# A graph layer on one core: projections as three passes over 12-bit parts, inputs laid out transposed, the self projection kept in DRAM

## The reference

```python
Wi, Wj = W[:, :512], W[:, 512:]                 # W is 512 x 1024
mi = einsum('bkd,od->bko', x, Wi)               # x is 8 x 2048 x 512, float32
mj = einsum('bkd,od->bko', x, Wj)
a = adj.astype(float32)                         # adj is 2048 x 2048 int32, zeros and ones
deg = a.sum(axis=1)
out = deg[None, :, None] * (mi + b) + einsum('ij,bjo->bio', a, mj)
y = x + out
return (y - mean(y)) / sqrt(var(y) + 1e-5)      # over the last axis
```

## Time and profile before

| | |
|---|---|
| time, median of 3 runs (range) | 1845.88 us (1845.76 to 1846.46) |
| profiled execution, span from first to last instruction | 1843.9 us |
| what lies around the span (median less span) | 2.0 us |
| PE busy / DVE busy / ACT busy / POOL busy | 1826.7 / 1182.1 / 418.1 / 1.1 us |
| moved by DMA | 86.41 MB, 47 GB/s over the span |

### The profile page before, as it was taken

One profiled execution on the slowest core, in us unless ns is written; L12 is line 12 of the kernel. 1 busy time (PEld: TensorE's weight loads), 2 busy tenths in 40 slices (PEclk: granted clock), 3 DMA queues, 4 the chain that ended last, 5 costly groups with the idle time before them and its releaser, 6 DMA issues.

```text
span 1843.9 us, 20125 instructions
## 1 busy us (share of the span) xinstructions
PE 1826.7 (99%) x6352; PEld 1171.2 (64%) x6352; DVE 1182.1 (64%) x2704; ACT 418.1 (23%) x455; POOL 1.1 (0%) x8
## 2 busy tenths in 40 slices
PE   9999999999999999999999999999999999999998
PEld 5458854588545885458844688446884468844687
DVE  7755487645885558855588545875558844688454
ACT  4454410123001320022201222011220112211131
POOL 0000000000000000000000000000000000000000
PEclk9999999999999999999999999999999999999999
DMA  6530001100111001010101100010001100010001
GB/s 234 180 117 34 34 34 45 34 34 34 42 38 34 34 34 45 34 34 38 42 34 34 42 37 34 34 45 34 34 34 35 44 34 34 34 45 34 12 34 46
DMA packets 22765, 86.41 MB, mean 47 GB/s; under 512 B 2400, under 2 KB 3424, under 8 KB 20704
## 3 DMA queue, kind: packets, MB, share of 16 engines
q1 hardware_dynamic: 22752, 86.25, 12.9%
HBM read 52.69 MB, written 33.55 MB: 47 GB/s over the span
## 4 chain that ended last, share of the span: by engine, by line
PE 88%; DVE 9%; issue 2%; ACT 0%; DVEq 0%; DMA 0%; POOL 0%; POOLq 0%; SPq 0%
PE agg_ps L261 45%; PE mj_ps L243 21%; PE mi_ps L243 21%; DVE xT L402 5%; DVE stats L421 1%; DVE r L419 1%; DVE r L415 1%; PE aux_ps L234 0%; DVE r L410 0%; DVE newton L430 0%; PE mi_ps L304 0%; ACT std L340 0%; DVE mean_var L423 0%; DVE mj_top L388 0%; ACT WT L312 0%
## 5 line engine op out<-in xcount | busy, mean ns | idle before, releaser
L261 PE MATMUL agg_ps<-mj_hi,adjT 128*128 128x512 f32 x2048 | 799.7, 390 | 0.0
L261 PE MATMUL agg_ps<-mj_lo,adjT 128*128 128x512 f32 x2048 | 796.8, 389 | 0.0
L243 PE MATMUL mj_ps<-WT,xT 128*128 128x512 f32 x1024 | 461.9, 594 | 8.2 <-DVE xT L402 7.4
L243 PE MATMUL mi_ps<-WT,xT 128*128 128x512 f32 x1024 | 460.4, 592 | 0.8 <-ACT WT L312 0.8
L402 DVE STREAM_TRANSPOSE xT<-x_in 32x256 f32<-32x256 f32 x1008 | 439.2, 436 | 20.2 <-DMA x_in<-in_x 5.4
L261 PEld LDWEIGHTS agg_ps<-mj_hi,adjT 128*128 128x128 f32 x2048 | 384.4, 188 | 81.3 <-issue 1.7
L261 PEld LDWEIGHTS agg_ps<-mj_lo,adjT 128*128 128x128 f32 x2048 | 384.4, 188 | 81.3 <-issue 1.7
L334 ACT ACTIVATE adjT<-adjT 128x2048 fp32r (+1 forms) x128 | 244.4, 1915 | 548.1 <-PE agg_ps L261 548.0
L243 PEld LDWEIGHTS mi_ps<-WT,xT 128*128 128x128 f32 x1024 | 194.5, 190 | 245.5 <-issue 238.9
L243 PEld LDWEIGHTS mj_ps<-WT,xT 128*128 128x128 f32 x1024 | 192.1, 190 | 246.5 <-issue 245.3
L419 DVE TENSOR_TENSOR r<-agg_ps,r 128x512 f32 (+1 forms) x128 | 88.5, 691 | 345.9 <-PE agg_ps L261 345.4
(11 more groups left out here) (28 smaller groups left out, 172.6 us busy)
## 6 DMA issues: line engine op xcount, KB each, us to landing
x_in<-in_x SPq DMA_DIRECT2D x63, 512.0 KB, 3.3
out<-r SPq DMA_DIRECT2D x63, 512.0 KB, 2.6
stage<-in_adj SPq DMA_DIRECT2D x16, 1024.0 KB, 5.1
stage<-in_L_gnn_W SPq DMA_DIRECT2D x2, 512.0 KB, 5.2
stage<-in_L_gnn_W SPq DMA_DIRECT2D x1, 1024.0 KB, 9.4
x_in<-in_x SPq DMA_DIRECT2D x2, 256.0 KB, 4.6
out<-r SPq DMA_DIRECT2D x2, 256.0 KB, 2.0
bias<-in_L_gnn_b SPq DMA_DIRECT2D x1, 256.0 KB, 9.5
```

The source lines that it names most:

```text
L243: last = nc.tensor.matmul(dst[u % 2][:, :], xT[u // 2][:, u % 2, k, :], WT[:, half * DK + k, :], start=(k == 0), stop=(k == DK - 1))
L261: last = nc.tensor.matmul(agg_ps[s][:, :], adjT[s][:, j, :], part[:, j, :], start=(j == 0 and part is mj_hi), stop=(j == NT - 1 and part i ...
```

## The change

**Projection.** `x`, W and their parts are handled in 12-bit pieces. For a tile, `x_top` is the upper bits of x, `x_hi` the same as fp32r, `x_lo` is 4096 times the rest, and `x_df = x_top - x_lo`; for W the parts are `W_hi`, `W_lo` and `W_df`. A product is then `main * (1 + 1/4096) - cross`, where `main` sums `x_hi * W_hi` and `x_lo * W_lo` (8 matmuls) and `cross` sums `x_df * W_df` (4 matmuls). All operands are fp32r, so `mj` and `mi` of a tile take 24 matmul instructions. DVE makes the top and the rest (`split_x`) and combines (`combine_mj`, `combine_mi`); ACT makes `x_hi` and `x_lo` (`parts`), copies `cross` out of PSUM (`take_cross`) and makes `mj_hi`; POOL makes `x_df` (`difference`) and `mj_lo` (`rest_of_mj`). `x_top`, `mj` and `mi` have one buffer each.

**Layout.** The host hands over `x` once as it is and once transposed by tile (`xt`), `adj` transposed in blocks of 128 x 512 (`adjt`, 64 chunks) and W transposed (`wt`, 8 chunks). No engine transposes any more. Of the chunks of `adj`, 32 are handled in the projection stage of batch 0, two a tile, and 32 in its aggregation stage: 3 in each of tiles 1 to 4, 2 in tiles 5 and 6, 4 in tiles 7 to 10. DVE counts the degrees of each chunk and ACT casts it.

**Self projection.** `mi` is stored to `mi_dram` a tile at a time and read back in the aggregation stage, where POOL adds the bias (`add_bias`) and DVE forms `r = mi * deg + x` (`residual`). `r` now has four single-tile buffers, and `x` is read a second time into them. All transfers are of 256 KB and all are issued by SP.

In the cut below the new parts come in the order SP, POOL, PE, ACT, DVE, host.

```diff
-            def project(n, u, dst, half, free, ready, wait_free):
...
-                    last = nc.tensor.matmul(dst[u % 2][:, :], xT[u // 2][:, u % 2, k, :], WT[:, half * DK + k, :],
-                                            start=(k == 0), stop=(k == DK - 1))
-                last.then_inc(ready, 1)
...
-            def transpose_pair(q, slot, quadrants, slot_value):
...
-                for a in quadrants:
-                    blocks = x_in[slot][a * B:(a + 1) * B, :, :].rearrange("p s (k g c) -> p s k g c", g=Q, c=B)
-                    for g in range(Q):
-                        last = nc.vector.transpose(xT[slot][g * B:(g + 1) * B, :, :, a * B:(a + 1) * B],
-                                                   blocks[:, :, :, g, :])
...
-            def residual(n, t, u):
-                dve.wait_ge(mi_ready, n + 1)
-                nc.vector.scalar_tensor_tensor(slot(r, t), mi_ps[u % 2][:, :], deg[:, bass.ds(t, 1)],
-                                               x_in[u // 2][:, u % 2, :], ALU.mult, ALU.add).then_inc(r_ready, 1)
...
-                nc.vector.scalar_tensor_tensor(slot(r, i), bias[:, :], deg[:, bass.ds(i, 1)], slot(r, i),
-                                               ALU.mult, ALU.add).then_inc(degb_ready, 1)
...
+            def load_chunk(c):
+                s = c % 2
+                if c >= 2:
+                    sp.wait_ge(adj_cast, c - 1)
+                    sp.wait_ge(deg_part_ready, c - 1)
+                sp.dma_start(adj_in[s][:, :], adjt[c // NT, c % NT]).then_inc(adj_loaded[s], 16)
+            sp.dma_start(x_raw[0][:, :], xt[0]).then_inc(x_loaded[0], 16)
+            for c in range(DK, 2 * DK):
+                sp.dma_start(w_stage[c][:, :], wt[c]).then_inc(w_loaded[c], 16)
+            sp.dma_start(x_raw[1][:, :], xt[1]).then_inc(x_loaded[1], 16)
+            for c in range(DK):
+                sp.dma_start(w_stage[c][:, :], wt[c]).then_inc(w_loaded[c], 16)
...
+            def load_mi(m, u):
+                sp.dma_start(mi_in[u % 2][:, :], mi_dram[m]).then_inc(mi_loaded[u % 2], 16)
+            def load_r(m, u, turn):
+                if turn is not None:
+                    sp.wait_ge(out_stored[u], turn)
+                sp.dma_start(r[u][:, :], x_tiles[m]).then_inc(r_loaded[u], 16)
...
+                def proj(g):
+                    for u in range(GT):
+                        n = NT * bt + GT * g + u
+                        last = final and known(g) and g == NG - 1
+                        if not (last and u >= GT - 2):
+                            sp.wait_ge(x_parts_ready, 2 * n + 2)
+                            sp.dma_start(x_raw[u % 2][:, :], xt[n + 2]).then_inc(x_loaded[u % 2], 16)
+                        if zero:
+                            for c in range(PROJ_CHUNKS * (GT * g + u), PROJ_CHUNKS * (GT * g + u + 1)):
+                                load_chunk(c)
+                        sp.wait_ge(mi_ready, n + 1)
+                        sp.dma_start(mi_dram[n], mi[:, :]).then_inc(mi_stored, 16)
+                over_groups(sp, zero, final, proj)
+                base = NT * bt
+                sp.wait_ge(mi_stored, 16 * (base + 2))
+                for u in range(2):
+                    load_mi(base + u, u)
+                for u in range(GT):
+                    load_r(base + u, u, None if zero else 16 * NG * bt)
+                def agg(g):
+                    for u in range(GT):
+                        i = GT * g + u
+                        m = base + i
+                        ending = known(g) and g == NG - 1
+                        if zero:
+                            for c in agg_chunks(i):
+                                load_chunk(c)
+                        sp.wait_ge(norm_ready, m + 1)
+                        sp.dma_start(out_tiles[m], r[u][:, :]).then_inc(out_stored[u], 16)
+                        if not (ending and u >= GT - 2):
+                            sp.wait_ge(mi_stored, 16 * (base + NT))
+                            load_mi(m + 2, u)
+                        if not ending:
+                            load_r(m + GT, u, 16 * (NG * bt + g + 1))
...
+            def difference(n, s):
+                pool.wait_ge(x_parts_ready, 2 * n + 2)
+                pool.tensor_tensor(x_df[s][:, :], x_top[:, :], x_lo[s][:, :].bitcast(fp32),
+                                   ALU.subtract).then_inc(x_df_ready, 1)
+            def rest_of_mj(n, t):
+                pool.wait_ge(mj_hi_ready, n + 1)
+                pool.tensor_tensor(mj_lo[:, bass.ds(t, 1), :].rearrange("p t d -> p (t d)"), mj[:, :],
+                                   mj_hi[:, bass.ds(t, 1), :].rearrange("p t d -> p (t d)").bitcast(fp32),
+                                   ALU.subtract).then_inc(mj_lo_ready, 1)
+            def add_bias(m, u, turn):
+                pool.wait_ge(mi_loaded[u % 2], turn)
+                pool.tensor_tensor(mi_in[u % 2][:, :], mi_in[u % 2][:, :], bias[:, :], ALU.add).then_inc(mib_ready, 1)
...
+                        if not (final and known(g) and g == NG - 1 and u == GT - 1):
+                            difference(n + 1, (u + 1) % 2)
+                        rest_of_mj(n, GT * g + u)
...
+                with pool.Fori(0, NP) as k:
+                    for u in range(2):
+                        add_bias(NT * bt + 2 * k + u, u, 16 * (NP * bt + k + 1))
...
+            def project(n, s, h, first):
+                half = 1 - h
...
+                if h == 0:
+                    pe.wait_ge(x_df_ready, n + 1)
+                if not first:
+                    pe.wait_ge(cross_ready, 2 * n - 1 + h)
+                    last = nc.tensor.matmul(cross_ps[h][:, :], x_df[s][:, k * P:(k + 1) * P],
+                                            W_df[:, half * DK + k, :], start=(k == 0), stop=(k == DK - 1))
+                last.then_inc(cross_done, 1)
...
+                if not first:
+                    pe.wait_ge(mj_ready if h == 0 else mi_ready, n)
+                    nc.tensor.matmul(main_ps[h][:, :], x_hi[s][:, k * P:(k + 1) * P],
+                                     W_hi[:, half * DK + k, :], start=(k == 0), stop=False)
+                    last = nc.tensor.matmul(main_ps[h][:, :], x_lo[s][:, k * P:(k + 1) * P],
+                                            W_lo[:, half * DK + k, :], start=False, stop=(k == DK - 1))
+                last.then_inc(main_done, 1)
...
+            def parts(n, s):
+                act.wait_ge(x_top_ready, n + 1)
+                if not (known(n) and n < 2):
+                    act.wait_ge(main_done, 2 * n - 2)
+                nc.scalar.activation(x_hi[s][:, :], x_top[:, :], ACT.Copy).then_inc(x_parts_ready, 1)
+                act.wait_ge(x_rest_ready, n + 1)
+                nc.scalar.activation(x_lo[s][:, :], x_raw[s][:, :], ACT.Copy, scale=S).then_inc(x_parts_ready, 1)
+            def take_cross(n, h):
+                act.wait_ge(cross_done, 2 * n + 1 + h)
+                if not (known(n) and n == 0):
+                    act.wait_ge(mj_ready if h == 0 else mi_ready, n)
...
+                nc.scalar.activation(cross[h][:, :], cross_ps[h][:, :], ACT.Copy).then_inc(cross_ready, 1)
+            def top_of_mj(n, t):
+                act.wait_ge(mj_ready, n + 1)
+                nc.scalar.activation(mj_hi[:, bass.ds(t, 1), :].rearrange("p t d -> p (t d)"), mj[:, :],
+                                     ACT.Copy).then_inc(mj_hi_ready, 1)
+            def cast_chunk(c):
+                s = c % 2
+                act.wait_ge(adj_loaded[s], 16 * (c // 2 + 1))
...
+                nc.scalar.activation(adjT8[:, j, q * DO:(q + 1) * DO], adj_in[s][:, :], ACT.Copy).then_inc(adj_cast, 1)
+            def widen(i, s, chunks):
+                if chunks is not None:
+                    act.wait_ge(adj_cast, chunks)
+                nc.scalar.activation(adjT[s][:, :, :], adjT8[:, :, bass.ds(i * P, P)], ACT.Copy).then_inc(adjT_ready, 1)
...
+                        if not (final and known(g) and g == NG - 1 and u == GT - 1):
+                            parts(n + 1, (u + 1) % 2)
+                        take_cross(n, 0)
+                        if zero:
+                            cast_chunk(PROJ_CHUNKS * t)
+                        take_cross(n, 1)
+                        top_of_mj(n, t)
+                        if zero:
+                            cast_chunk(PROJ_CHUNKS * t + 1)
+                for i in range(2):
+                    widen(i, i, NT if zero else None)
...
+            def split_w(c, order):
...
+                dve.wait_ge(w_loaded[c], 16)
...
+                nc.vector.tensor_scalar(top[:, :].bitcast(u32), w_stage[c][:, :].bitcast(u32),
+                                        HI_BITS, None, ALU.bitwise_and).then_inc(w_top_ready, 1)
+                dve.wait_ge(w_top_ready, order + 1)
+                nc.vector.tensor_tensor(W_lo[:, c, :], w_stage[c][:, :], top[:, :], ALU.subtract).then_inc(w_lo_ready, 1)
...
```

(138 more changed lines are left out.)

431 lines of the change are left out of this document (204 added, 227 removed).

## The result

The changed kernel takes 1937.24 us (1936.61 to 1938.41, 4 runs) against 1846.16 for the kernel before: ratio 1.0494, 95% interval 1.048 to 1.0509. It is slower by 4.9%. The forecast was 1965, range 1880 to 2070. The profiled execution has a span of 1934.5 us.

The account below looks back on a forecast made before the run. PE bounds the kernel before; afterwards late loads set the pace. Last aggregation starts at 403 + 6 x 235.0 = 1813; 146.7 to the last scaling and 2.5 for the store give span 1962, about 1965 us, range 1880 to 2070.

Parts of the forecast that it names:

- The bound: Before the change PE bounds the kernel, working 1826.7 of 1843.9 us; a batch costs 227.3 us.
- loop 1: Aggregation: normalise, SP, store's issue, late load of mi, POOL's addition, residual; 9.05 us a tile against PE's 7.26.
- P: Time of one aggregation tile through normalise, load of mi, POOL and residual: 9.05 us, bounds 7.7 to 10.1.
- 7.36 + 15P: Start of a batch's last addition, counted from the start of its aggregation: 143.1 us.
- Loop 2: Projection: the load of x waits behind mi_ready and a store, then split and combine_mi; 5.68 us a tile against PE's 5.45.
- Handover: Between aggregation and next projection: PE idles 9.5 us at the second tile; a batch takes 235.0 us against 227.3.
- Batch 0: Aggregation starts at 124; tiles of 13.8 us with 3 chunks, 14.5 with 4, 11.0 with 2; 180 us where 15P is 136.
- Rival 1: Aggregation loop short enough to keep PE's saving, faster from P = 7.95 down: 1765 to 1840 us, chance 9%.
- Rival 2: PE's clock falls to 1.2 GHz at handovers, 32 us, or through aggregation, over 500 us; chance 9% above 30 us.
- rival 3: POOL and DVE block each other in the projection: up to 1.17 us a tile, 115 us, giving 2080; chance 6%.
- any clock but 1.00: Sign on PE that the forecast is wrong; the granted clock was 1.00 throughout the kernel before.

Follow-up runs that it names:

- experiment 1: Changed kernel with the load of mi for tile m+2 issued after the residual of tile m, ahead of the wait for its normalisation: 1762.28 us.
- experiment 3: Changed kernel without POOL's addition of the bias, the residual waiting for the load itself: 1797.01 us in one run.
- experiment 2: Changed kernel with the load of mi issued ahead of the store of the normalised tile, still behind norm_ready: 1920.10 us.
- experiment 5: experiment 1 plus batch 0's aggregation chunks of adj loaded a tile ahead into four buffers: 1692.62 us, 0.9162 of the kernel before.
- experiment 6: Changed kernel with chunks a tile ahead in four buffers, the load of mi left where the change put it: 1890.25 us in one run.
- experiment 4: Changed kernel without the four matmuls of x_lo by W_lo in each projection half: 1937.15 us in one run.
- experiment 8: experiment 5 plus the load of x a tile earlier, and without the x_lo by W_lo matmuls: 1530.26 us in one run.

## Why the prediction was right

**The bound and loop 1.** Right in mechanism: experiments 1 and 3 show the chain through the late load, link by link. P was 9.24 in the tile shown and 9.21 on average, against 9.05. The terms that were off: store's issue to load's issue 0.65, 0.57 on average, and not 0.40 (a pair of issues at the start of the kernel was the wrong row; with no wait between them, in experiment 2, two issues in the loop are still 0.52 apart), and POOL with wake 1.44 against 1.25. The load was 2.69, on average 2.73, against 2.83: the 0.1 that the forecast added for the store ahead had no row behind it, and it did not show.

**The number of periods.** This is the step that failed. "The last at 7.36 + 15P" counts one P too many: the last tile of a batch has no residual ahead of it, and its addition follows the one before by 3.6 us (537.76 to 541.64 is 3.9, 769.21 to 772.82 is 3.6).

```profile
537.76 0.68 DVE L534 TENSOR_TENSOR r<-agg_ps,r 128x512 f32<-128x512 f32 x1
```

A batch has 14 P and 3.6 to 3.9. One period fewer, -5.4 us, and the longer P (9.21 on average), +2.2, make 3.2 us of the 3.4 by which a cycle was overestimated, and the miscount is the 5.4 in the last row of the table. The rest of a cycle, from the last addition of a batch to the first of the next, was forecast at 99.3 us and took 99.1 on average. That is in part luck, for in batch 2 its parts are off by more: the main half of `mi` starts 1.2 us later than forecast, the way from there to the first matmul of aggregation is 3.2 shorter, and the first addition comes 1.7 later.

**Loop 2.** Forecast 5.68, in fact 5.4, level with PE's 5.44. In one tile of the kernel after (`combine_mi` at 626.71 and at 632.10) the combine took 0.69 (forecast 0.75), SP up to the load's issue 0.65 (0.62), the load 2.98 (2.83), the top 0.46 (0.55), the rest 0.61 (0.69, and 0.16 for gaps), 5.39 in all. The largest difference is in the gaps: a successor on DVE starts before its predecessor's recorded end.

**Handover.** Right in kind, but the idle time of PE was half as long. The timeline of the end of batch 1:

```profile
541.64 0.69 DVE L534 TENSOR_TENSOR r<-agg_ps,r 128x512 f32<-128x512 f32 x1
...
543.61 0.20 ACT L409 ACTIVATE std<-var_eps 128x1 f32<-128x1 f32 x1 [3.30 <-DVE var_eps L540]
...
545.57 1.27 POOL L245 TENSOR_TENSOR x_df<-x_top,x_lo 128x512 fp32r<-128x512 f32 x1 [8.51 <-ACT x_lo L380]
...
546.97 2.07 PE L293 MATMUL cross_ps<-W_df,x_df 128*128 128x512 f32 x4 [4.40 <-POOL x_df L245]
```

PE idles 4.4 us, not 9.5, as the last addition comes 5.4 us earlier than thought. One wait was not foreseen: at the start of the stage the first residual waits for x in `r`, the fourth of seven transfers issued together. The first addition is at 640.64 although PE began the stage at 631.55 and so was done 7.3 us later; some 1.7 us a batch.

```profile
639.15 1.57 DVE L528 SCALAR_TENSOR_TENSOR r<-mi_in,deg,r 128x512 f32<-128x512 f32 x2 [6.37 <-DMA r<-in_x]
```

The widening ahead of the stage cost 1.27 us on PE, as forecast (1.3).

**Batch 0.** The sum was right to 1 us from first addition to first addition, in part by luck: tiles with three chunks took 13.5 to 13.8 us, the first of them 15.7 (forecast 13.8), those with four 14.5 to 15.0 (14.5), two tiles behind them 11.5 and 10.1 (9.05), and the superfluous P made up for it. That its excess is round trips is shown by experiments 5 and 6.

**The rivals.** Rival 1 did not come: P would have had to be below 7.95. It gave 1765 us for additions as PE alone allows them; experiment 1, with additions 7.25 us apart, took 1762. Rival 2, the clock, came in a mild form. The four matmuls after the idle of 4.4 us took 2.07 us, elsewhere 1.07, and the stretch 546 to 550 has a mean granted clock of 0.57: the 1.2 GHz level for part of it. In batch 2 it costs little, as the main half of `mi` starts at 552.15 where `mi` allows it from 551.33: at most 0.8 us. In batches 4 to 6, after idles of 4.2 us, the low level lasted longer (a mean of 0.50 over 1008 to 1014), and that half starts 2.0 to 2.2 us late. (The one 8 of the PEclk row behind batch 0 is 1209 to 1257, with such a handover.) The second `combine_mi` came 6.2 to 6.6 us after the first there, 5.4 in batch 2, and POOL (rival 3) has a part in that. So clock and POOL together cost such a batch 0.8 to 1.2 us more than batch 2. In aggregation PE waits 1 to 2 us a tile, and the granted clock over 640 to 760 is 0.97 on average: of its twelve stretches of 10 us, two fell to 0.84 and 0.83 (680 to 690, 730 to 740), one to 0.98. That costs little too, since a tile there waits for DVE anyway. In the aggregation of batch 0 it fell further, to 0.67 over 190 to 210 and to 0.58 over 250 to 270, where PE was not the bound. The prediction had named any clock but 1.00 as a sign of being wrong. The sign came, and the time was right because PE was not what the stages waited for. Rival 3 came too, and cost little. In batch 0 POOL works from 26.96 to 28.25, and a count on DVE with two SBUF inputs that begins meanwhile takes 1.39 us and not 0.69:

```profile
26.96 1.29 POOL L245 TENSOR_TENSOR x_df<-x_top,x_lo 128x512 fp32r<-128x512 f32 x1 [0.35 <-ACT x_lo L380]
27.41 1.39 DVE L514 TENSOR_TENSOR deg_part<-deg_part,adj_in 128x512 f32<-128x512 f32 x1
```

It ends at 28.80, 0.55 us after POOL. By the Trainium skill ("SBUF — State Buffer", its text on the shared port pair) a VectorE operation with two SBUF inputs and a GpSimd one that reads SBUF lock each other out; the trace agrees. The 60 such counts have a mean of 0.95 us, so 60 x 0.25 = 15 us of DVE; all the long ones lie before 120 us, where DVE was busy 77% of the time, and how much of them reached the total was not tested. In the later batches the subtraction in `split_x` (mean 0.70) was spared but for one of 1.67. The step ahead of it was not, although it has one SBUF input: of the 110 `x_top` of batches 1 to 7, 55 took more than 0.45 us, up to 1.53 where the others took 0.43 to 0.45, and each of the 55 ended 0.27 to 0.29 us after POOL's `mj_lo`:

```profile
1016.70 1.29 POOL L250 TENSOR_TENSOR mj_lo<-mj,mj_hi 128x512 f32 x1 [2.30 <-ACT mj_hi L393]
1016.74 1.53 DVE L479 TENSOR_SCALAR x_top<-x_raw 128x512 uint32<-128x512 uint32 x1 [1.57 <-DMA x_raw<-in_xt]
```

That is 11 us of DVE in all, in loop 2. The forecast had ruled this out by saying that POOL is done before x lands; in these tiles it was not.

## What to carry to other kernels

Prefetch distance is where the issue stands in program order, not the number of buffers: a load issued behind the end of tile m-1 and needed ahead of tile m makes a loop of normalise, issue, landing, helper and residual, 9.24 us where PE needs 7.26, and moving one line took 175 us off. Before pricing a saving on the busiest engine, write down for each stage the shortest such loop through SP; two loops may be level with the engine, and then cutting its work by a third gives nothing until the loop is opened (0 us in experiment 4, 169 in experiment 8). Count the periods at the ends of a loop, where one wait falls away, and check what a moved wait does in the stage with other loads on the same queue: the same edit gained in seven batches and lost 11 us in one.

## What the runs showed of the hardware

- An idle of 4.4 us on PE was enough for its next matmuls to run at the 1.2 GHz level for a part: four took 2.07 us in place of 1.07. After the seven handovers (idles of 3.9 to 4.4 us, one of 2.1) the first four took 2.07 us five times, 1.60 and 1.19. With waits of 1 to 2 us a tile in aggregation the clock mostly stayed at 1.00, but fell to 0.84 and 0.83 in two of twelve stretches of 10 us. The timeline of the kernel after shows the first fall, behind a wait of 1.82 us: starts that were 0.23 us apart are 0.43 apart for 3 us, then 0.22 again.

```profile
678.51 0.50 PE L327 MATMUL agg_ps<-mj_hi,adjT 128*128 128x512 f32 x1 [1.82 <-DVE r L534]
...
679.08 0.40 PE L327 MATMUL agg_ps<-mj_hi,adjT 128*128 128x512 f32 x1
679.32 0.39 PE L327 MATMUL agg_ps<-mj_lo,adjT 128*128 128x512 f32 x1
...
680.68 0.63 PE L327 MATMUL agg_ps<-mj_lo,adjT 128*128 128x512 f32 x1
681.10 0.63 PE L327 MATMUL agg_ps<-mj_hi,adjT 128*128 128x512 f32 x1
...
683.19 0.39 PE L327 MATMUL agg_ps<-mj_lo,adjT 128*128 128x512 f32 x1
683.41 0.39 PE L327 MATMUL agg_ps<-mj_hi,adjT 128*128 128x512 f32 x1
```

- A POOL `tensor_tensor` of 128x512 float32 took 1.29 us, 1.9 times DVE's 0.69.
- A bitwise operation of 128x512 from SBUF to SBUF on DVE took 0.42 us alone (the splits of W); the same from PSUM 0.69.
- DVE operations with one SBUF input were held by POOL as well as those with two. `x_top` took up to 1.53 us in place of 0.43. In experiment 1, where POOL's additions fall beside the normalisation, 26 of the 128 scalings (L553) took 1.4 to 1.7 us in place of 0.55, and each of these ended 0.28 to 0.29 us after POOL's addition.
- A 256 KB load was in use 2.73 us after its issue on average, with a store issued 0.57 us ahead of it, and 2.96 with the store issued 0.52 us behind it.
